# Sparse attention with new orders on four engines, transposes issued one item early, and a bias moved from a one-row product to VectorE

## The chip, the cores and the metric

The kernel runs on one core of a Trainium2 chip. The metric is the device time of one execution in microseconds (us). The core has four engines that compute, each with its own instruction queue, executed in order: TensorE (PE; its weight loads are listed as PEld), VectorE (DVE), ScalarE (ACT) and GpSimd (POOL). SyncE (SP) issues transfers, and so does GpSimd for gathers by index. The engines meet only through semaphores: an instruction waits until a counter has reached a value, and an instruction that is done raises one.

## The reference

4096 tokens of width 128 (16 sequences of 256) pass through four layers, each with a residual sum and a layer norm in front: a linear attention, a mixture of 8 experts (each token goes to one of them), a sparse attention, and the same mixture once more. The sparse attention is the part that changes:

```python
Q, K = (_rope(Q), _rope(K))
iq = (x @ w_iq.T + b_iq).reshape(B, S, IDX_HEADS, IDX_DIM)
ik = x @ w_ik.T + b_ik
iw = x @ w_iw.T + b_iw
head_scores = jax.nn.relu(jnp.einsum('bqhd,bkd->bhqk', iq, ik))
index_scores = jnp.einsum('bhqk,bqh->bqk', head_scores, iw)
_, top_idx = jax.lax.top_k(index_scores, k)      # k = 32 of 256 keys
logits = jnp.einsum('bqd,bkd->bqk', Q, K) * scale + attn_bias   # -inf off the top 32
attn_out = jnp.einsum('bqk,bkd->bqd', softmax(logits), V)
return attn_out @ w_o.T + b_o
```

`iw` has four values per token, one for each index head. Its bias `b_iw` is what the change adds on another engine.

## The kernel before

All data is float32. The program has five stages: the linear attention (to about 85 us), routing and experts (to 204 us), the sparse attention (212 to about 415 us), routing and experts again (to the end). The sparse attention handles one sequence of 256 tokens (two tiles of 128 rows, index `c`) at a time, as a software pipeline written out by hand. In step `b` the engines work on several items at once, and the order in each queue is the order of the source:

- GpSimd (lines 477 to 496) gathers rows of item `b+2` by index (L447, two transfers of 128 rows), multiplies queries and keys of item `b` by cosine and sine (L481, L483), adds them (`qr`, L488), adds the first two weighted heads of each tile (`head_sum`, L466, twice, called heads 0 and heads 1 below), takes the inverse deviation of a later item (`inverse_std`: `vpe` L458 and `rs` L460), and adds an output bias to X (L493).
- VectorE finds the top 32 by four rounds of a maximum of 8 and a replacement (L1329, L1332). Ahead of the rounds it adds the third and fourth head (L1274, L1280) and masks the logits (L1288). Between the rounds stand small pieces of other items (`beside`): after round 0 the normalised rows `xf` of item `b-3` (L1262) and the shift `nb` of item `b+1` (L1237), which both wait for `rs`, after round 2 the attended rows.
- ScalarE copies projections out of PSUM (L888, with `vb` in L891 and `iw` in L915), takes the exponentials (L901), normalises rows of item `b+1` (`xb`, L864, which waits for `nb`), copies scores through a relu (L927, two pairs, called relu 0 and relu 1 below), and scales two heads by `iw` (L934, called part 0 and part 1).
- TensorE transposes `xb` (L691), projects (L660, L663), makes `iw` with a one-row product of ones and the bias row `rowc` (L712) and two products (L714), multiplies probabilities and values (L724), and makes the index scores (L679, two sets of four products). A relu copy waits for its set of scores (`idx`).

So item `b+1` is normalised in step `b`, and before it is projected it must be transposed by TensorE and copied to `xbT` by ScalarE (L872). X and its normalised rows leave through SP (L341, L343).

The expert stages run 39 incidences of a tile with an expert. VectorE and ScalarE fetch tile and expert numbers into registers in groups of eight, where `opens(st, lag)` (line 306) says so. With lag 2, as on VectorE, it holds in steps 2, 8, 16, 24, 32 and 40 of 41; the load at 32 fetches nine numbers, which last to the end.

Of the kernel before, what the change touches and what calls it, by code (L numbers as in the profile page):

```python
# [10 lines left out]
ALU = mybir.AluOpType  # L11
# [3 lines left out]
P = 128  # L15
# [104 lines left out]
def build(nc, x, w_attn, w_idx, w_experts, b1_cols, b2, w_router, cols, b_out, b_o, b_iw, b_r, consts, out):  # L120
    with ExitStack() as ctx:  # L121
# [28 lines left out]
        rowc = sb("rowc", [1, C * IDX_HEADS])  # L150
# [155 lines left out]
        def opens(st, lag):  # L306

            return (st.base - HEAD) % TURN == 0 or st.base == lag or st.base == T
# [5 lines left out]
        def _(sp):  # L314
# [11 lines left out]
            for c in range(C):  # L326
                sp.dma_start(rowc[:, c * IDX_HEADS:(c + 1) * IDX_HEADS], b_iw).then_inc(ld_w, 16)
# [42 lines left out]
        def _(pool):  # L370
# [31 lines left out]
            for st in steps(pool, B, 3, 7, 4, ahead=1):  # L402
                if st.base in GROUP_STEPS and st.on(-1, B):
                    deviations(GROUP_STEPS[st.base])
                if st.on(1, B):
                    b, r = st.item(1), st.slot(1, 2)
                    pool.wait_ge(ld_w, 80)
# [69 lines left out]
            for s in range(B + 2):  # L477
                b, r = s, s % 2
                if b < B:
                    pool.wait_ge(b_["pje"], 8 * b + 7)  # L480
# [4 lines left out]
                    add_heads(b, r, 0)  # L485
                    pool.wait_ge(b_["rp"], 2 * (b + 1))
                    after(pool, b_["S"], C * (b - 1))
                    pool.tensor_tensor(qr[r][:, :, :], qk[r][:, 0:2, :], qk[r][:, 2:4, :], ALU.add).then_inc(b_["qr"], 1)  # L488
                    add_heads(b, r, 1)
                inverse_std(s)  # L490
                if b < B:
                    pool.wait_ge(b_["xb"], b + 1)
                    pool.tensor_tensor(X[:, b * C:(b + 1) * C, :], X[:, b * C:(b + 1) * C, :],  # L493
                                       bo_bc[:, :].unsqueeze(1).to_broadcast([P, C, D]), ALU.add).then_inc(b_["xo"], 1)
                if b + 3 < B:
                    gather_x(b + 3)
# [4 lines left out]
        def _(pe):  # L501
# [26 lines left out]
            for st in steps(pe, B, 6, 7, 4, ahead=1):  # L528
# [18 lines left out]
                if st.base == 6:  # L547
                    pe.wait_ge(ld_w, 80)
# [102 lines left out]
            keep_clock(KEEP_GATHER, bank[4][:, 0:P])  # L651
            for st in (Step(s) for s in range(B + 4)):
# [32 lines left out]
                if st.on(0, B):  # L685
                    b, r = st.item(0), st.slot(0, 2)
                    pe.wait_ge(b_["xb"], b + 1)
                    after(pe, b_["iwe"], b)
                    after(pe, tails[1]["xfT"], b - 3)
                    for c in range(C):  # L690
                        mm = pe.transpose(bank[5][:, c * P:(c + 1) * P], xb[r][:, c, :], ident)  # L691
                    mm.then_inc(b_["T"], 1)
# [34 lines left out]
                if st.on(0, B):  # L727
                    index_scores(0)
# [17 lines left out]
        def _(act):  # L746
# [129 lines left out]
            for st in (Step(s) for s in range(B + 4)):  # L876
# [41 lines left out]
                if st.on(-1, B):  # L918
                    normalise_b(st, -1)
# [469 lines left out]
```

## Time and profile before

| | |
|---|---|
| median of 3 runs | 567.39 us (567.18 to 570.19) |
| the profiled execution | 566.95 us, of it the span of its records 565.1 us |
| busy, share of the span | PE 451.0 us (80%), DVE 380.0 (67%), ACT 337.2 (60%), POOL 288.4 (51%) |
| mean granted clock of TensorE | 0.922 |
| sparse attention | about 212 to 415 us, 16 steps and the run-out |

Most rows of the next section but one are of the timeline: start in us from the start of the span, duration, engine, source line, operation, output and inputs, sizes, number of instructions merged in the row, and in brackets how long the engine was idle before and who ended it. An engine starts an instruction a little before the one ahead is recorded as done, so ends and starts overlap by up to 0.1 us.

### The profile page before, as it was taken

The numbers are of one execution on the slowest core, as the hardware profiler recorded it, in microseconds if no ns is written. First come the engines' busy times: TensorE is split into PE (matmuls) and PEld (weight loads), VectorE is DVE, ScalarE is ACT, GpSimd is POOL, SyncE is SP. The second block draws the span as 40 slices with busy tenths as digits, with TensorE's granted clock in tenths as the row PEclk, the third lists the DMA queues.
The fourth block names the chain that finished last, engine by engine and source line by source line (L and its number), as shares of the span: only waits on it lengthen the run. The fifth ranks groups of instructions, "written<-read, shape, count | busy, mean of one in ns | idle before, by whom it ended". The sixth has DMA issues, their size and how long they took to land. (4 is left out here: it accounts for less than half of the span.)

```text
span 565.1 us, 11633 instructions
## 1 busy us (share of the span) xinstructions
PE 451.0 (80%) x3048; PEld 390.7 (69%) x3048; DVE 380.0 (67%) x1501; ACT 337.2 (60%) x934; POOL 288.4 (51%) x329
## 2 busy tenths in 40 slices
PE   1789985859999986999889998889647668786991
PEld 1578865859999874676666766667437568676981
DVE  5789976425666622999999999999957234434661
ACT  1568852226776616889999899998521245434650
POOL 5753440454430025987778777775410633665442
PEclk9989995979999989999999999999756969888996
DMA  8942232131331110011111111110111321121110
GB/s 224 288 135 77 74 90 25 44 88 53 99 87 35 34 34 15 9 37 32 28 30 30 42 44 28 30 30 21 36 35 5 84 57 48 56 64 56 39 36 17
DMA packets 45070, 32.42 MB, mean 57 GB/s; under 512 B 13524, under 2 KB 39508, under 8 KB 45012
## 3 DMA queue, kind: packets, MB, share of 16 engines
q1 hardware_dynamic: 39892, 19.11, 12.2%
q0 software_dynamic: 5120, 12.62, 8.5%
q8 instruction: 26, 0.43, 0.3%
q14 instruction: 32, 0.26, 0.2%
HBM read 19.10 MB, written 12.62 MB: 56 GB/s over the span
## 5 line engine op out<-in xcount | busy, mean ns | idle before, releaser
L629 PE MATMUL bank<-X,w 128*128 x624 | 91.0, 292 | 18.3 <-ACT X L834 16.3
L639 PE MATMUL bank<-WE,hT 128*128 x624 | 89.2, 289 | 14.3 <-ACT hT L847 6.8
L427 POOL DMA_INDIRECT big<-rows,gidx x64 | 61.5, 961 | 74.7 <-DVE gidx L1147 28.2
L629 PEld LDWEIGHTS bank<-X,w 128*128 128x128 f32 x624 | 82.0, 205 | 22.3 <-issue 21.9
L639 PEld LDWEIGHTS bank<-WE,hT 128*128 128x128 f32 x624 | 81.3, 203 | 17.0 <-issue 16.9
L834 ACT ACTIVATE X<-bank 128x128 f32<-128x128 f32 x64 | 17.9, 280 | 94.6 <-PE bank L620 60.9
L1179 DVE TENSOR_SCALAR hT<-bank,w 128x128 f32<-128x128 f32 x156 | 47.6, 346 | 39.0 <-issue 12.2
L660 PE MATMUL bank<-xbT,WB 128*128 128x256 f32 x224 | 59.2, 394 | 13.2 <-ACT xbT L872 8.5
L839 ACT ACTIVATE w<-WE 128x644 f32 x78 | 57.5, 738 | 3.1 <-DVE big L1191 2.8
L847 ACT ACTIVATE hT<-bank,w 128x128 f32<-128x128 f32 x156 | 48.7, 367 | 13.4 <-PE bank L629 10.1
L447 POOL DMA_INDIRECT X<-x,pidx x32 | 31.7, 989 | 48.7 <-DMA x<-big 41.2
L660 PEld LDWEIGHTS bank<-xbT,WB 128*128 128x128 f32 x224 | 38.7, 189 | 25.2 <-ACT iq L888 11.1
L1332 DVE MATCH_REPLACE8 wk<-m,wk 128x256 f32<-128x256 f32 x128 | 51.8, 416 | 0.0
L433 POOL DMA_INDIRECT out<-big,gidx x32 | 31.4, 980 | 38.1 <-DVE big L1191 32.5
L1329 DVE MAX8 m<-wk 128x8 f32<-128x256 f32 x128 | 47.9, 419 | 0.0
L1185 DVE TENSOR_TENSOR yb<-bank,w 128x128 f32<-128x128 f32 x78 | 22.6, 289 | 36.3 <-PE bank L639 20.4
L1191 DVE SCALAR_TENSOR_TENSOR big<-yb,gm,big 128x128 f32 x78 | 27.5, 353 | 16.4 <-DVE yb L1185 12.1
L679 PE MATMUL bank<-ik,iq 64*128 64x256 f32 x256 | 37.8, 402 | 0.7 <-ACT big L927 0.7
L466 POOL TENSOR_TENSOR head_sum<-big 128x256 f32<-128x256 f32 x32 | 23.6, 736 | 27.9 <-ACT big L934 27.8
L927 ACT ACTIVATE big<-bank 128x512 f32<-128x512 f32 x64 | 34.7, 594 | 1.1 <-PE bank L679 0.9
L888 ACT ACTIVATE big<-bank,COL 128x256 f32<-128x256 f32 x64 | 29.4, 496 | 0.8 <-PE bank L660 0.7
L934 ACT ACTIVATE big<-big,iw 128x256 f32<-128x256 f32 x64 | 29.3, 511 | 0.6
(161 smaller groups left out, 1026.6 us busy)
## 6 DMA issues: line engine op xcount, KB each, us to landing
WE<-w_experts SPq DMA_DIRECT2D x2, 2048.0 KB, 11.5
rows<-xf SPq DMA_DIRECT2D x32, 128.0 KB, 2.2
rows<-X SPq DMA_DIRECT2D x32, 128.0 KB, 2.7
X<-x SPq DMA_DIRECT2D x4, 512.0 KB, 7.6
x<-big SPq DMA_DIRECT2D x32, 64.0 KB, 1.5
big<-rows,gidx POOLq DMA_INDIRECT x64
WB<-w_idx SPq DMA_DIRECT2D x1, 640.0 KB, 5.7
WE<-b SPq DMA_DIRECT2D x1, 512.0 KB, 12.9
```

The source lines that it names most:

```text
L427: pool.indirect_dma_start(xg[:, j, :], None, rows_dram[n], bass.IndirectOffsetOnAxis(ap=gidx[:, j:j + 1], axis=0)).then_inc(f["g"][j % G_R ...
L447: pool.indirect_dma_start(X[:, t, :], None, x2_dram, bass.IndirectOffsetOnAxis(ap=pidx[:, t:t + 1], axis=0)).then_inc(b_["x"][r], 16)
L629: mm = pe.matmul(bank[r + 2 * (k // 2)][:, k % 2 * P:(k % 2 + 1) * P], w1[st.slot(1, 4)][:, k * P:(k + 1) * P], moving, start=True, stop=True)
L639: mm = pe.matmul(bank[4 + r][:, 0:D], hT[r][:, k, :], WE[:, bass.ds(expert[(s - 2) % TURN], 1), W2_AT + k * D:W2_AT + (k + 1) * D].rearran ...
L660: mm = pe.matmul(to, WB[:, i * D:(i + 1) * D], xbT[r][:, :], start=True, stop=True)
L679: mm = pe.matmul(bank[h % 2][:, h // 2 * S:(h // 2 + 1) * S], iq[r][lo:lo + IDX_DIM, h // 2, c * P:(c + 1) * P], ik[r][lo:lo + IDX_DIM, :] ...
L839: act.activation(w1[st.slot(0, 4)][:, :], WE[:, bass.ds(expert[st.base], 1), 0:W1_LEN].rearrange("p a w -> p (a w)"), ACT.Copy).then_inc(f ...
L847: act.activation(hT[r][:, k, :], bank[r][:, k * P:(k + 1) * P], ACT.Relu, bias=w1[st.slot(1, 4)][:, B1_AT + k:B1_AT + k + 1]).then_inc(f[" ...
L927: act.activation(rel[r][:, c, i::2, :], bank[i][:, :].rearrange("p (h k) -> p h k", h=2), ACT.Relu).then_inc(b_["rel"], 1)
L1179: dve.tensor_scalar(hT[r][:, k, :], bank[2 + r][:, k % 2 * P:(k % 2 + 1) * P], w1[st.slot(1, 4)][:, B1_AT + k:B1_AT + k + 1], 0.0, ALU.add ...
L1329: dve.max(m8[:, c, :], wk[r][:, c, :]).then_inc(b_["v"], 1)
L1332: dve.match_replace(wk[r][:, c, :], m8[:, c, :], wk[r][:, c, :], NEG).then_inc(b_["v"], 1)
```

## The change

- GpSimd: in step `s` the gather for item `s+3`, the inverse deviation of step `s-1` and the bias sum of item `s` come first. Then cosine, sine and `qr`, and both head sums last. Before, the head sums stood around `qr`, and inverse deviation, bias sum and gather (of item `s+3`) ended the step.
- TensorE: the transposes of `xb` for item `b+1` go to bank 4 instead of bank 5, and stand in step `b` between the product of probabilities and values and the first set of index scores. Before, they opened step `b+1`, behind the second set.
- ScalarE: in the last pair of projections the `vb` copy comes after the normalisation of item `b+1` and not before it. `xbT` is copied ahead of relu 1 and not behind it. The `iw` copy is gone.
- `iw` is now VectorE's: `index_weights` adds a bias that was broadcast to all partitions, after round 1. The one-row product is gone.
- `opens` holds for steps up to 32 only, so that the load at step 40 of an expert stage falls away on VectorE.

```diff
-            return (st.base - HEAD) % TURN == 0 or st.base == lag or st.base == T
+            return st.base <= T and ((st.base - HEAD) % TURN == 0 or st.base == lag or st.base == T)
...
-            for c in range(C):
-                sp.dma_start(rowc[:, c * IDX_HEADS:(c + 1) * IDX_HEADS], b_iw).then_inc(ld_w, 16)
+            sp.dma_start(biw_bc[:, :], b_iw.rearrange("a e -> (a e)").partition_broadcast(P)).then_inc(ld_w, 16)
...
             for s in range(B + 2):
                 b, r = s, s % 2
+                if b + 3 < B:
+                    gather_x(b + 3)
+                if s > 0:
+                    inverse_std(s - 1)
                 if b < B:
+                    pool.wait_ge(b_["xb"], b + 1)
+                    pool.tensor_tensor(X[:, b * C:(b + 1) * C, :], X[:, b * C:(b + 1) * C, :],
+                                       bo_bc[:, :].unsqueeze(1).to_broadcast([P, C, D]), ALU.add).then_inc(b_["xo"], 1)
                     pool.wait_ge(b_["pje"], 8 * b + 7)
...
-                    add_heads(b, r, 0)
                     pool.wait_ge(b_["rp"], 2 * (b + 1))
                     after(pool, b_["S"], C * (b - 1))
                     pool.tensor_tensor(qr[r][:, :, :], qk[r][:, 0:2, :], qk[r][:, 2:4, :], ALU.add).then_inc(b_["qr"], 1)
+                    add_heads(b, r, 0)
                     add_heads(b, r, 1)
-                inverse_std(s)
-                if b < B:
-                    pool.wait_ge(b_["xb"], b + 1)
-                    pool.tensor_tensor(X[:, b * C:(b + 1) * C, :], X[:, b * C:(b + 1) * C, :],
-                                       bo_bc[:, :].unsqueeze(1).to_broadcast([P, C, D]), ALU.add).then_inc(b_["xo"], 1)
-                if b + 3 < B:
-                    gather_x(b + 3)
+            inverse_std(B + 1)
...
+            def turn_rows(b, r):
+
+                pe.wait_ge(b_["xb"], b + 1)
+                for c in range(C):
+                    mm = pe.transpose(bank[4][:, c * P:(c + 1) * P], xb[r][:, c, :], ident)
+                mm.then_inc(b_["T"], 1)
+
+            turn_rows(0, 0)
...
-                if st.on(0, B):
-                    b, r = st.item(0), st.slot(0, 2)
-                    pe.wait_ge(b_["xb"], b + 1)
-                    after(pe, b_["iwe"], b)
-                    after(pe, tails[1]["xfT"], b - 3)
-                    for c in range(C):
-                        mm = pe.transpose(bank[5][:, c * P:(c + 1) * P], xb[r][:, c, :], ident)
-                    mm.then_inc(b_["T"], 1)
...
-                    pe.matmul(bank[5][:, S:S + C * IDX_HEADS], ones[0:1, :], rowc[:, 0:C * IDX_HEADS], start=True, stop=False)
+                    after(pe, tails[1]["xfT"], b - 3)
...
+                if st.on(-1, B):
+                    turn_rows(st.item(-1), st.slot(-1, 2))
                 if st.on(0, B):
                     index_scores(0)
...
                 if st.on(0, B):
-                    projected(3)
-                    act.wait_ge(b_["pj"], 5 * (b + 1))
-                    after(act, b_["wk"], C * (b - 1))
-                    act.activation(iw[r][:, :, :],
-                                   bank[5][:, S:S + C * IDX_HEADS].rearrange("p (c h) -> p c h", c=C),
-                                   ACT.Copy).then_inc(b_["iwe"], 1)
+                    projected(3, (0,))
                 if st.on(-1, B):
                     normalise_b(st, -1)
+                if st.on(0, B):
+                    projected(3, (1,))
...
-                    if c == C - 1 and st.on(-1, B):
-                        turned(st.item(-1), st.slot(-1, 2))
...
+                    if c == 0 and st.on(-1, B):
+                        turned(st.item(-1), st.slot(-1, 2))
...
+            def index_weights(b, r):
+
+                dve.wait_ge(b_["pj"], 5 * (b + 1))
+                dve.tensor_tensor(iw[r][:, :, :], bank[5][:, S:S + C * IDX_HEADS].rearrange("p (c h) -> p c h", c=C),
+                                  biw_bc[:, :].unsqueeze(1).to_broadcast([P, C, IDX_HEADS]), ALU.add).then_inc(b_["iwe"], 1)
...
+                    if i == 1 and st.on(0, B):
+                        index_weights(st.item(0), st.slot(0, 2))
```

On GpSimd, a middle step of the attention and the opening of the next read so before (`big` is where queries, keys and weighted heads lie, `pidx` the gather's indices):

```order
L466 TENSOR_TENSOR head_sum<-big 128x256 [waits b_s1,b_prt]
L488 TENSOR_TENSOR qr<-big 128x512 [waits b_S,b_rp]
L466 TENSOR_TENSOR head_sum<-big 128x256 [waits b_s1,b_prt]
L458 TENSOR_TENSOR vpe_1<-mv_1,eps 128x4 [waits b_xb,b_mv]
L460 TENSOR_TENSOR rs_1<-vpe_1,mhalf 128x4 [waits b_ve]
L493 TENSOR_TENSOR X<-X,bo_bc 128x256 [waits b_xb]
L447 DMA X<-x,pidx 128x128 [waits b_x0]
L447 DMA X<-x,pidx 128x128
L481 TENSOR_TENSOR big<-big,cst 128x512 [waits b_pje]
L483 TENSOR_TENSOR big<-big,cst 128x512
```

And in the changed kernel, from the same sums on (its line numbers differ):

```order
L493 TENSOR_TENSOR qr<-big 128x512 [waits b_S,b_rp]
L465 TENSOR_TENSOR head_sum<-big 128x256 [waits b_s1,b_prt] x2
L446 DMA X<-x,pidx 128x128 [waits b_x0]
L446 DMA X<-x,pidx 128x128
L457 TENSOR_TENSOR vpe_0<-mv_0,eps 128x4 [waits bt_xf,b_xb,b_mv]
L459 TENSOR_TENSOR rs_0<-vpe_0,mhalf 128x4 [waits b_ve]
L484 TENSOR_TENSOR X<-X,bo_bc 128x256 [waits b_xb]
L487 TENSOR_TENSOR big<-big,cst 128x512 [waits b_pje]
L489 TENSOR_TENSOR big<-big,cst 128x512
```

The two gathers have moved ahead of `vpe` and `rs`, and `qr` ahead of both head sums.

On TensorE, the end of the projections of a middle step before (`prT` are the transposed probabilities, `ik` and `iq` the index keys and queries):

```order
L712 MATMUL bank<-rowc,cst 128x8
L714 MATMUL bank<-WB,xbT 128x4 x2
L724 MATMUL bank<-vb,prT 128x128 [waits bt_lg,bt_x,b_prT]
L724 MATMUL bank<-vb,prT 128x128 x3
L679 MATMUL bank<-ik,iq 128x256 [waits b_rel] x2
L679 MATMUL bank<-ik,iq 128x256 x2
L734 MATMUL bank<-qr 128x256 [waits b_ttr,b_qr]
L734 MATMUL bank<-qr 128x256
```

The same place in the changed kernel:

```order
L714 MATMUL bank<-WB,xbT 128x4 [waits bt_xfT]
L714 MATMUL bank<-WB,xbT 128x4
L724 MATMUL bank<-vb,prT 128x128 [waits bt_lg,bt_x,b_prT]
L724 MATMUL bank<-vb,prT 128x128 x3
L656 MATMUL bank<-cst,xb 128x128 [waits b_xb]
L656 MATMUL bank<-cst,xb 128x128
L687 MATMUL bank<-ik,iq 128x256 [waits b_rel] x2
L687 MATMUL bank<-ik,iq 128x256 x2
L736 MATMUL bank<-qr 128x256 [waits b_ttr,b_qr]
L736 MATMUL bank<-qr 128x256
```

The one-row product is gone, and the transposes of `xb`, which wait for ScalarE's `xb`, stand ahead of the first scores.

On ScalarE, from the seventh projection to part 1 before:

```order
L888 ACTIVATE big<-bank,COL 128x256 [waits b_pj]
L891 ACTIVATE vb<-bank 128x256 [waits b_PV]
L915 ACTIVATE iw<-bank 128x8 [waits b_wk,b_pj]
L864 ACTIVATE xb<-X,nb,rs_1 128x128 [waits b_T,b_nb]
L864 ACTIVATE xb<-X,nb,rs_1 128x128
L927 ACTIVATE big<-bank 128x2x256 [waits b_idx,b_iwe,b_hs]
L927 ACTIVATE big<-bank 128x2x256 [waits b_idx]
L934 ACTIVATE big<-big,iw 128x256 [waits b_rel]
L934 ACTIVATE big<-big,iw 128x256
L751 ACTIVATE xfT<-bank 128x256 [waits bt_T]
L927 ACTIVATE big<-bank 128x2x256 [waits b_idx] x2
L872 ACTIVATE xbT<-bank 128x256 [waits b_idx,b_T]
```

And in the changed kernel:

```order
L890 ACTIVATE big<-bank,COL 128x256 [waits b_pj]
L866 ACTIVATE xb<-X,nb,rs_1 128x128 [waits b_T,b_nb]
L866 ACTIVATE xb<-X,nb,rs_1 128x128
L893 ACTIVATE vb<-bank 128x256 [waits b_PV,b_pj]
L926 ACTIVATE big<-bank 128x2x256 [waits b_idx,b_iwe,b_hs]
L926 ACTIVATE big<-bank 128x2x256 [waits b_idx]
L931 ACTIVATE big<-big,iw 128x256 [waits b_rel]
L931 ACTIVATE big<-big,iw 128x256
L874 ACTIVATE xbT<-bank 128x256 [waits b_idx,b_T]
L753 ACTIVATE xfT<-bank 128x256 [waits bt_T]
L926 ACTIVATE big<-bank 128x2x256 [waits b_idx] x2
```

`xb` now precedes `vb`, the `iw` copy is gone, and `xbT` (L874 there) stands between part 0 and relu 1.

## Rows read from the trace of the kernel before

**Rows 1.** Windows of the attention stage, 240 to 300 us: length, busy time (count).
```profile
240.00:300.00 60.00, 54.03 (x324) 41.15 (x322) 56.75 (x238) 53.10 (x145) 47.36 (x51) 1.00 0.13 31
```

**Rows 2.** Timeline, ScalarE in one step: start us, duration us, line, tiles, idle before.
```profile
302.24 1.09 ACT L927 ACTIVATE big<-bank 128x512 f32<-128x512 f32 x2
...
303.36 0.91 ACT L934 ACTIVATE big<-big,iw 128x256 f32<-128x256 f32 x2
...
304.50 1.09 ACT L927 ACTIVATE big<-bank 128x512 f32<-128x512 f32 x2
...
305.47 0.39 ACT L872 ACTIVATE xbT<-bank 128x256 f32<-128x256 f32 x1
...
305.74 0.92 ACT L934 ACTIVATE big<-big,iw 128x256 f32<-128x256 f32 x2
...
311.58 0.47 ACT L888 ACTIVATE big<-bank,COL 128x256 f32<-128x256 f32 x1
...
312.94 0.39 ACT L891 ACTIVATE vb<-bank 128x256 f32<-128x256 f32 x1 [0.88 <-PE bank L724]
...
313.28 0.88 ACT L864 ACTIVATE xb<-X,nb,rs 128x128 f32<-128x128 f32 x2
...
314.08 1.09 ACT L927 ACTIVATE big<-bank 128x512 f32<-128x512 f32 x2
```

**Rows 3.** Timeline, TensorE before and after that copy (PE, and PEld for weight loads).
```profile
312.83 1.13 PE L679 MATMUL bank<-ik,iq 64*128 64x256 f32 x8
...
316.49 0.20 PEld L691 LDWEIGHTS bank<-cst,xb 128*128 128x128 f32 x2 [0.55 <-issue]
```

**Rows 4.** Timeline of the first steps: TensorE's scores and the ScalarE copies.
```profile
221.06 1.13 PE L679 MATMUL bank<-ik,iq 64*128 64x256 f32 x8
...
222.28 1.09 ACT L927 ACTIVATE big<-bank 128x512 f32<-128x512 f32 x2 [0.17 <-PE bank L679]
...
231.69 1.09 ACT L927 ACTIVATE big<-bank 128x512 f32<-128x512 f32 x2 [0.16 <-issue]
...
243.26 1.09 ACT L927 ACTIVATE big<-bank 128x512 f32<-128x512 f32 x2
```

**Rows 5.** Timeline, GpSimd in the same step.
```profile
305.04 1.27 POOL L488 TENSOR_TENSOR qr<-big 128x512 f32<-128x512 f32 x1
...
306.73 0.73 POOL L466 TENSOR_TENSOR head_sum<-big 128x256 f32<-128x256 f32 x1 [0.43 <-ACT big L934]
...
307.70 1.19 POOL L460 TENSOR_TENSOR rs<-vpe,mhalf 128x4 f32<-128x4 f32 x1
...
308.88 0.82 POOL L493 TENSOR_TENSOR X<-X,bo_bc 128x256 f32<-128x256 f32 x1
...
309.87 1.04 POOL L447 DMA_INDIRECT X<-x,pidx  x1 [0.17 <-issue]
...
312.19 1.28 POOL L481 TENSOR_TENSOR big<-big,cst 128x512 f32<-128x512 f32 x1
```

**Rows 6.** Timeline, VectorE in the same step.
```profile
305.56 1.02 DVE L1274 SCALAR_TENSOR_TENSOR wk<-big,iw,head_sum 128x256 f32<-128x256 f32 x1
...
307.50 0.48 DVE L1274 SCALAR_TENSOR_TENSOR wk<-big,iw,head_sum 128x256 f32<-128x256 f32 x1
...
310.47 0.60 DVE L1262 TENSOR_SCALAR xf<-X,mv,rs 128x128 f32<-128x128 f32 x2
...
310.97 0.17 DVE L1237 SCALAR_TENSOR_TENSOR nb<-mv,rs 128x2 f32<-128x2 f32 x1
```

**Rows 7.** Timeline of the first stage, VectorE beside GpSimd.
```profile
40.66 1.00 DVE L1012 TENSOR_SCALAR xa<-X,mv,r 128x128 f32<-128x128 f32 x2
...
40.84 0.74 POOL L409 TENSOR_TENSOR xres<-xres,bout_bc 128x256 f32<-128x256 f32 x1 [2.36 <-ACT xres L783]
```

**Rows 8.** Timeline, end of the first expert stage.
```profile
199.63 2.24 PE L639 MATMUL bank<-WE,hT 128*128 x16
...
203.40 0.16 DVE L1171 TENSOR_TENSOR gm<-big,mine 128x1 f32<-128x1 f32 x1 [1.82 <-issue]
```

More of the change, by code:

```diff
@@ L149, in build @@
         bv_rep = sb("bv_rep", [P, P])
-        rowc = sb("rowc", [1, C * IDX_HEADS])
+        biw_bc = sb("biw_bc", [P, IDX_HEADS])
         br_bc = sb("br_bc", [P, E])
@@ L406, in _ @@
                     b, r = st.item(1), st.slot(1, 2)
-                    pool.wait_ge(ld_w, 80)
+                    pool.wait_ge(ld_w, 64)
                     pool.wait_ge(a_pt, b + 1)
@@ L547, in _ @@
                 if st.base == 6:
-                    pe.wait_ge(ld_w, 80)
+                    pe.wait_ge(ld_w, 64)
                 if st.on(6, B):
@@ L711, in _ @@
                     b, r = st.item(0), st.slot(0, 2)
-                    pe.matmul(bank[5][:, S:S + C * IDX_HEADS], ones[0:1, :], rowc[:, 0:C * IDX_HEADS], start=True, stop=False)
+                    after(pe, tails[1]["xfT"], b - 3)
                     for c in range(C):
                         mm = pe.matmul(bank[5][:, S + c * IDX_HEADS:S + (c + 1) * IDX_HEADS], xbT[r][:, c * P:(c + 1) * P],
-                                       WB[:, 9 * D:9 * D + IDX_HEADS], start=False, stop=(c == C - 1))
+                                       WB[:, 9 * D:9 * D + IDX_HEADS], start=True, stop=True)
                     mm.then_inc(b_["pj"], 1)
@@ L871, in turned @@
                 after(act, b_["idx"], 2 * C * (b - 1))
-                act.activation(xbT[r][:, :], bank[5][:, 0:S], ACT.Copy).then_inc(b_["xbT"], 1)
+                act.activation(xbT[r][:, :], bank[4][:, 0:S], ACT.Copy).then_inc(b_["xbT"], 1)
             normalise_b(Step(0), 0)
@@ L877, in _, with projected @@
                 b, r = st.item(0), st.slot(0, 2)
-                def projected(pair):
+                def projected(pair, which=(0, 1)):
                     act.wait_ge(b_["pj"], 5 * b + pair + 1)
-                    for i in (2 * pair, 2 * pair + 1):
+                    for i in (2 * pair + w for w in which):
                         src = bank[2 + pair % 2][:, i % 2 * S:(i % 2 + 1) * S]
```

## Prediction

> **What bounds the kernel now.** I read the busy windows first, then the timeline of one step, engine by engine, and followed which event released which. In the attention stage no engine is idle for long: of 60 us DVE is busy 56.8, PE 54.0, ACT 53.1, POOL 47.4, at full clock [rows 1]. So a step is set by a loop of waits. Its length is the distance between two relu 0 copies: 302.24 to 314.08, that is 11.84 us [rows 2]; I read the same distance from step to step in the middle of the stage. All times t below count from relu 0.
>
> In this step ACT waits 0.88 us ahead of `vb` (t = 10.70), runs `xb`, 0.88 long, from 11.04 to 11.92, and goes straight on with the next relu 0 [rows 2]. The reader is to see that TensorE is no slower. Its first scores begin at 312.83, 1.25 us ahead of relu 0 [rows 3], and in the first step, where ACT waited for them, the distance was 1.22 [rows 4]. Both ways to relu 0 end within 0.03 us.
>
> POOL has slack: `rs` is ready at 308.89, but DVE comes to `xf` at 310.47, and `nb` is done at 311.14, 2.1 us ahead of its reader `xb` at 313.28 [rows 2, 5, 6].
>
> **The change part by part.** First the gain that is visible. With `vb` behind `xb`, `xb` could use the wait of 0.88 us, if `nb` is there. It would need `nb` by t = 9.8 (end of the seventh projection: 311.58 + 0.47, t = 9.81 [rows 2]).
>
> Then what stands in its way. The chain is now relu 0, part 1, heads 1, gather, `rs`, `xf` and `nb`, `xb`, transposes, scores, next relu 0. Every link is a wait or an order in the queue rows of the changed kernel, and all of it lies within one step. Its length, link by link:
>
> - Relu 0 to the end of part 1: 306.66 - 302.24 = 4.42 before. Part 0 begins 1.12 after relu 0, but part 1 begins 1.24 after relu 1, with `xbT` in between [rows 2]. Moved ahead, `xbT` costs its 0.27 (305.47 to 305.74) before relu 1, and part 1 then follows at 1.12. That is 0.15 more: 4.57.
> - Heads 1 begins 0.07 later and takes 0.73; two gathers follow, with 0.17 ahead of the first (309.70 to 309.87) and 2.32 from there to the next operation (312.19). `vpe` and `rs` end 1.43 after heads 1 in the old order, so I take 1.47 behind a gather with its start [rows 5]. Sum 4.76: `rs` is ready at t = 9.33. Before it was ready at 6.65.
> - A wait of 0.03, then `xf` and `nb`, 310.47 to 311.14: 0.67 [rows 6]. Then `xb` with 0.04 + 0.88.
> - Transposes: about 0.05 until they start and 0.25 of TensorE's time, by their 0.20 of weight loads [rows 3]. Then 1.22 from scores to relu 0 [rows 4].
>
> Sum: 9.33 + 0.70 + 0.92 + 0.30 + 1.22 = 12.47 us for a step, 0.63 longer than now, with no contention at all.
>
> Next, contention between DVE and POOL. A sum of two SBUF tensors on DVE (L1274) took 1.02 us beside POOL's `qr`, and 0.48 later in the same step, beside `vpe` and the start of `rs`, which have only four elements a row. It ended at 306.58, 0.27 after `qr` [rows 5, 6]. In the first stage a pair of L1012, the same operation as `xf` and of the same size, took 1.00 instead of `xf`'s 0.60 beside a POOL sum [rows 6, 7]. The Trainium skill, "SBUF — State Buffer", section "Who interferes with whom", says that this port pair is an exclusive lock and not a shared bandwidth; by that rule, the trace agrees. Today `xf` meets only a gather, and POOL's bias sum (308.88) is over by then. In the changed order `rs` is followed on POOL by this very sum, at t = 9.31. `xf` arrives at 9.36 and waits until the sum ends, about 10.04 (0.73, as heads 1). The first half of `xf` is done 0.08 later (as 41.66 after 41.58 [rows 7]), the second 0.26 later, `nb` 0.07 after that: 10.45 instead of 10.03. The step is then 12.88 us, 1.04 longer than now. I take this value; without the lock it is 0.63. On the gain side, `qr` no longer holds up L1274, 0.54 us per step on DVE, and hidden, since DVE then has time to spare: it is busy for 56.8 of 60 us [rows 1], so 11.2 of a step, less 0.54, plus some 0.1 for `index_weights`: 10.8 against 12.9.
>
> Without the gather, in steps 13 and 14, the way over TensorE decides: transposes in front of the scores (0.25) and the 0.15 above, on a path that had 0.03 to spare. That is 0.4 per step. The removed one-row product lies in front of the product with the probabilities, which waits for the `prT` copy anyway. I cost it at nothing; without that cover it would give back up to 0.2 a step, since it is about as large as the pair of transposes. The `iw` copy stands in the 0.34 between `vb` and `xb` and is worth 0.1 at most. DVE's replacement comes long before TensorE and ACT ask for it. The weights of `b_iw` need one transfer instead of two, long before use: nothing.
>
> Steps at the start: relu 0 stood 9.41 and 11.57 us apart in steps 1 and 2 (222.28, 231.69, 243.26 [rows 4]), without ACT's `xfT` copy and with shorter `rs`. The new chain is shorter there too, by about 1.0, so about 11.9: 2.5 more in step 1 and 0.4 in step 2 (12.9 at most, the full chain; 11.3 at least, without the lock). Step 0 now has `xb` of item 1 ahead of its first scores: 0.8, an estimate between 0.3 (the transposes alone) and 1.2 (`xb` in full). Step 3 is 1.2 longer, since the distance before was still a little short.
>
> The sum: 0.8 + 2.5 + 0.4 + 1.2 + 9 x 1.04 (steps 4 to 12) + 2 x 0.4 = 15.1 us more.
>
> The load that falls away in `opens`: at the end of an expert stage DVE sat idle for 1.82 us ahead of the last gating product, at 203.40, while TensorE's last products had ended at 199.63 + 2.24 = 201.87. The following sum of the expert bias needs only these, and started 0.08 after 203.40. So it starts 1.6 us earlier [rows 8]. The second expert stage ends with the same pattern: two places, 3.2 us less. It can be 0, if something else ends as late; nothing in the rows says so, since the stores and the last scatter wait for this very result.
>
> Together 15.1 - 3.2 = 11.9 us more. The profiled execution took 566.95 us with a span of 565.1; the median of the runs is 0.44 above it. 567.39 + 11.9 = 579.3, so 579.
>
> **The rivals.** Half a per cent (2.8 us) is about what a measurement can tell from no change.
>
> - No contention: the chain is right but `xf` and `nb` slip in beside the bias sum. 0.8 + 1.9 + 0 + 0.8 + 9 x 0.63 + 0.8 = 10.0, less 3.2: 574. Against it stand rows 5 to 7.
> - The lock is taken again between the halves. POOL's cosine product is ready when the seventh projection is out (t = 9.81 + 0.15, plus 0.07), just when the bias sum ends at 10.04. In the first stage the POOL sum started 0.18 after the pair of DVE, and the pair still ended only with it, so it went between the two halves [rows 7]. If cosine (1.28 [rows 5]) gets in between the halves of `xf`, the step is 14.0, ten steps give about 11 more: 590. If sine then gets in before `nb`, 15.2 and 602. The Trainium skill, "SBUF — State Buffer", section "SBUF: two separate sides", says that the one that starts first holds the pair for its whole instruction; this fits either order and would give 579 to 602.
> - Faster, on the other side: `nb` comes in time, `xb` fills ACT's 0.88 us, and the transposes hide. This decides if `rs` is ready by t = 9.1 less the lock, and if the scores start no later than now. A step of 11.2 over 13 steps gives 8 less, with 3.2 from the load: 556. For it speaks that the idle time is real; against it that the gathers alone add 2.5 us to a path with 2.1 us of slack, and that TensorE had 0.03.
> - The terms cancel, within half a per cent: the transposes cost nothing, the gathers overlap with waits, and only the start loses: about 568.
>
> **How the numbers follow.** One lock per step, 579: 0.38. No contention, 574: 0.14. Cosine in between, 590: 0.18. Sine too, 602: 0.10. Faster, 556: 0.14. Cancelling: 0.06. The range 571 to 603 holds the first four, 0.80. Slower by over half a per cent is their sum too.
>
> **What would show it.** Right: relu 0 every 12.9 us in steps 3 to 12 and every 12.2 in 13 and 14; ACT's `xb` waits for `nb`, and PE's transposes for `xb`; `xf` about 1.0 long right behind `rs`, with two gathers ahead of `vpe`; L1274 back at 0.48; the last gating product of both expert stages right behind TensorE. Wrong: `xb` starting without a wait, or `xf` at 0.6 (574), or 2.3 and more (590 on). If relu 0 comes sooner than 12.4 after the last, one of the links above is not serial.

## Result and the profile after

The changed kernel takes 623.64 us (median of 4 runs, 621.44 to 625.38) against 567.28 us of the kernel before on the same chip (4 runs, 566.59 to 570.19): ratio 1.098, 95% interval 1.093 to 1.103. The direction was forecast, the size was not: 579 with a range to 603. The profiled execution took 623.91 us, span 622.0 us.

The page of the changed kernel: busy time, then two of its costliest groups (busy and mean ns of one, then idle time just before them and what ended it).

```profile
PE 471.9 (76%) x3016; PEld 400.3 (64%) x3016; DVE 397.7 (64%) x1517; ACT 339.0 (54%) x918; POOL 288.1 (46%) x329
...
L465 POOL TENSOR_TENSOR head_sum<-big 128x256 f32<-128x256 f32 x32 | 23.2, 725 | 83.9 <-ACT big L931 83.9
...
L866 ACT ACTIVATE xb<-X,nb,rs 128x128 f32<-128x128 f32 x32 | 14.0, 487 | 39.8 <-DVE nb L1236 39.8
```

POOL's and ACT's busy time stay as they were. PE is busy for 21 us more with 32 instructions fewer, DVE for 18 us more. So the time went into waits, into slower matmuls, and into something that counts as busy on DVE (below it turns out to be waiting inside instructions). The windows of the attention stage (length, busy us and count of PE, PEld, DVE, ACT, POOL, then the granted clock, DMA share, GB/s) show where:

```profile
240.00:300.00 60.00, 43.96 (x232) 32.03 (x232) 49.38 (x180) 41.71 (x108) 37.09 (x40) 0.92 0.09 23
300.00:360.00 60.00, 44.62 (x230) 32.65 (x227) 44.86 (x163) 39.20 (x103) 33.18 (x37) 0.86 0.08 23
360.00:420.00 60.00, 43.65 (x210) 31.04 (x211) 48.01 (x173) 36.08 (x93) 32.17 (x34) 0.80 0.09 25
```

Before, the first of these windows held 324 matmuls at clock 1.00 and no idle engine [rows 1]. Now it holds 232, every engine has slack, and the clock is below 1. The waits of the stage, 212 to 450 us (total us, times, longest):

```profile
POOL head_sum L465 <- ACT big L931: 82.2, 30, 4.6
ACT xb L866 <- DVE nb L1236: 39.8, 12, 11.2
...
ACT big L926 <- PE bank L687: 37.7, 26, 2.6
...
DVE xf L1267 <- POOL rs L459: 10.6, 10, 1.1
```

These waits are links of the forecast loop: part 1, `rs`, `nb`, `xb`, scores, relu. The timeline (start, duration, idle before) shows the end of the first expert stage and then one loop, from relu 0 at 314.64 to relu 0 at 330.81:

```profile
200.48 2.24 PE L639 MATMUL bank<-WE,hT 128*128 x16
...
202.75 0.29 DVE L1184 TENSOR_TENSOR yb<-bank,w 128x128 f32<-128x128 f32 x1 [0.26 <-PE bank L639]
203.25 0.35 DVE L1190 SCALAR_TENSOR_TENSOR big<-yb,gm,big 128x128 f32 x1 [0.20 <-DVE yb L1184]
...
312.45 2.08 PE L687 MATMUL bank<-ik,iq 64*128 64x256 f32 x8
...
314.64 1.08 ACT L926 ACTIVATE big<-bank 128x512 f32<-128x512 f32 x2 [2.59 <-PE bank L687]
...
324.02 1.05 POOL L459 TENSOR_TENSOR rs<-vpe,mhalf 128x4 f32<-128x4 f32 x1
...
325.05 0.71 POOL L484 TENSOR_TENSOR X<-X,bo_bc 128x256 f32<-128x256 f32 x1
...
325.20 1.87 DVE L1267 TENSOR_SCALAR xf<-X,mv,rs 128x128 f32<-128x128 f32 x2 [1.09 <-POOL rs L459]
...
325.74 1.25 POOL L487 TENSOR_TENSOR big<-big,cst 128x512 f32<-128x512 f32 x1
326.95 1.25 POOL L489 TENSOR_TENSOR big<-big,cst 128x512 f32<-128x512 f32 x1
326.99 1.23 DVE L1236 SCALAR_TENSOR_TENSOR nb<-mv,rs 128x2 f32<-128x2 f32 x1
...
328.26 0.88 ACT L866 ACTIVATE xb<-X,nb,rs 128x128 f32<-128x128 f32 x2 [2.67 <-DVE nb L1236]
...
329.19 0.44 PE L656 MATMUL bank<-cst,xb 128*128 128x128 f32 x2 [2.76 <-ACT xb L866]
...
329.56 1.13 PE L687 MATMUL bank<-ik,iq 64*128 64x256 f32 x8
...
330.81 1.09 ACT L926 ACTIVATE big<-bank 128x512 f32<-128x512 f32 x2 [1.40 <-PE bank L687]
```

Read this step against [rows 5, 6]. `xf` took 1.87 us and not 0.60: its second half began when the bias sum ended (L484, 325.76) and ended with cosine (L487). `nb`, two elements a row, took 1.23 us and not 0.17: it ended with sine (L489). Meanwhile TensorE stood idle for 2.76 us. The scores of one step took 2.08 us at the lower of the clock's two levels, 1.2 GHz (312.45), and those of the next 1.13 at the upper, 2.4 GHz (329.56).

The distances between relu 0 copies, in the order of the steps:

| step | 1 | 2 | 3 | 4 to 12 (mean) | 13 | 14 | 15 |
|---|---|---|---|---|---|---|---|
| before | 9.41 | 11.57 | 11.62 | 11.84 | 11.84 | 11.84 | 11.84 |
| forecast | 11.9 | 12.0 | 12.8 | 12.88 | 12.2 | 12.2 | |
| after | 12.11 | 13.35 | 15.85 | 16.92 (16.0 to 17.7) | 13.29 | 12.30 | 11.90 |

The last relu 0 stands 57.8 us later than before (454.73 against 396.95), 1.4 of it already at the first. So the loop takes 56.4 us longer, as much as the times differ by: the loss lies in this loop, and what changed outside of it cancels.

### The profile page after: what moved, and what is told of

Read it like the earlier page. It is cut to its first block and busy times, and to the rows that moved or that the text cites. A ratio compares the mean times of both kernels' runs of the same rounds, so it can differ in the third digit from the quotient of the medians.

```text
span 622.0 us, 11551 instructions
## 1 busy us (share of the span) xinstructions
PE 471.9 (76%) x3016; PEld 400.3 (64%) x3016; DVE 397.7 (64%) x1517; ACT 339.0 (54%) x918; POOL 288.1 (46%) x329
## 5 line engine op out<-in xcount | busy, mean ns | idle before, releaser
L629 PE MATMUL bank<-X,w 128*128 x624 | 89.4, 289 | 11.5 <-ACT X L836 7.6
L629 PEld LDWEIGHTS bank<-X,w 128*128 128x128 f32 x624 | 80.6, 202 | 15.7 <-issue 15.5
L446 POOL DMA_INDIRECT X<-x,pidx x32 | 34.3, 1073 | 47.3 <-DMA x<-big 39.8
L926 ACT ACTIVATE big<-bank 128x512 f32<-128x512 f32 x64 | 34.7, 595 | 38.4 <-PE bank L687 38.4
L687 PE MATMUL bank<-ik,iq 64*128 64x256 f32 x256 | 46.3, 482 | 0.7 <-ACT big L926 0.7
L1190 DVE SCALAR_TENSOR_TENSOR big<-yb,gm,big 128x128 f32 x78 | 27.5, 353 | 16.0 <-DVE yb L1184 12.3
L687 PEld LDWEIGHTS bank<-ik,iq 64*128 64x128 f32 x256 | 28.2, 232 | 12.1 <-issue 7.1
L866 ACT ACTIVATE xb<-X,nb,rs 128x128 f32<-128x128 f32 x32 | 14.0, 487 | 39.8 <-DVE nb L1236 39.8
```

Source lines behind the costliest of these rows:

```text
L446: pool.indirect_dma_start(X[:, t, :], None, x2_dram, bass.IndirectOffsetOnAxis(ap=pidx[:, t:t + 1], axis=0)).then_inc(b_["x"][r], 16)
L629: mm = pe.matmul(bank[r + 2 * (k // 2)][:, k % 2 * P:(k % 2 + 1) * P], w1[st.slot(1, 4)][:, k * P:(k + 1) * P], moving, start=True, stop=True)
L687: mm = pe.matmul(bank[h % 2][:, h // 2 * S:(h // 2 + 1) * S], iq[r][lo:lo + IDX_DIM, h // 2, c * P:(c + 1) * P], ik[r][lo:lo + IDX_DIM, :] ...
L926: act.activation(rel[r][:, c, i::2, :], bank[i][:, :].rearrange("p (h k) -> p h k", h=2), ACT.Relu).then_inc(b_["rel"], 1)
```

## The experiments

All experiments ran on other chips than the run above, where the kernel before takes 529 us. No trace of the kernel before was kept there. The version that differs from it in the bias alone (below) has steps of 11.83 us, as before. Its other stages are shorter: the first relu 0 stands at 210.12 and not 222.28, and 139.9 us follow the last and not 168.2. So the experiments are compared by ratio, and by step.

**The freed register load alone.** The kernel before with one edit:

```diff
-            return (st.base - HEAD) % TURN == 0 or st.base == lag or st.base == T
+            return st.base <= T and ((st.base - HEAD) % TURN == 0 or st.base == lag or st.base == T)
```

> The kernel before with the change of opens alone: VectorE makes no load at step 40 of the two expert stages. By my reading the last gating product of each stage starts 1.6 us earlier: 567.3 - 3.2 = 564 us. If something else ends as late, 567.

Measured: 526.45 us against 529.04, ratio 0.9945 (0.9919 to 0.9972), so 2.6 us less, with 3.2 inside the interval. The step stays at 11.83. The term was right, and it is the only part of the change that was seen to pay.

**The new GpSimd order alone.** The kernel before, with only GpSimd's queue of the changed kernel:

```diff
+                if b + 3 < B:
+                    gather_x(b + 3)
+                if s > 0:
+                    inverse_std(s - 1)
...
-                    add_heads(b, r, 0)
...
+                    add_heads(b, r, 0)
                     add_heads(b, r, 1)
-                inverse_std(s)
```

> The kernel before with the new order on GpSimd alone. Theory of the loop (heads 1, gather, rs, xf and nb taking turns with GpSimd's sums, xb, relu 0): rs is ready at t = 9.2 after relu 0, nb some 3.3 later because bias sum, cosine and sine get in between, xb follows, and relu 0 comes 0.8 after the start of xb without a transpose ahead of it. A step of about 13.5 us, so 567 + 10 x 1.6 + about 3 at the start = 586 us, xf near 1.9 us and nb near 1.2 us long. Rival, that the transposes ahead of the scores and not GpSimd's order carry the loss: 567 to 570 and xb without a wait.

Measured: ratio 1.021 (1.015 to 1.027). Steps 4 to 12 are 12.67 us on average and jump between 12.0 and 13.2 to 13.3. Two steps from its timeline, one of each kind:

```profile
332.49 0.72 POOL L485 TENSOR_TENSOR X<-X,bo_bc 128x256 f32<-128x256 f32 x1
...
332.69 0.86 DVE L1263 TENSOR_SCALAR xf<-X,mv,rs 128x128 f32<-128x128 f32 x2
...
333.34 1.34 POOL L488 TENSOR_TENSOR big<-big,cst 128x512 f32<-128x512 f32 x1
333.48 1.22 DVE L1238 SCALAR_TENSOR_TENSOR nb<-mv,rs 128x2 f32<-128x2 f32 x1
...
344.86 1.88 DVE L1263 TENSOR_SCALAR xf<-X,mv,rs 128x128 f32<-128x128 f32 x2
...
346.65 1.23 DVE L1238 SCALAR_TENSOR_TENSOR nb<-mv,rs 128x2 f32<-128x2 f32 x1
```

The 13.5 us expected were too much. In the first of the two steps, 0.13 us lie between the end of the bias sum (333.21) and cosine, which waits for the seventh projection (its copy ended at 333.27). The second half of `xf` is under way by then and ends at 333.55; here cosine pays, with 1.34 us instead of 1.26. Only `nb` meets a whole sum, and relu 0 comes at 335.52, 12.0 after the last. In the second step the projection is out before the bias sum ends, cosine follows at once (345.39), and `xf` and `nb` pay 1.3 and 1.1 us. What makes the steps alternate was not tried. Here relu 0 follows `xb` directly, 0.78 us after its start (334.74, 335.52), since the transposes still stand in the next step: the two parts of the change cost more together than each alone.

**The new orders with the old GpSimd queue.** The changed kernel, with GpSimd's queue as before:

```diff
-                if b + 3 < B:
-                    gather_x(b + 3)
-                if s > 0:
-                    inverse_std(s - 1)
...
+                inverse_std(s)
...
+                if b + 3 < B:
+                    gather_x(b + 3)
```

> The changed kernel with GpSimd in its old order; all else of the change stays. Theory of the loop: no gather ahead of rs, no sum beside xf, so only the transposes ahead of the scores and the copy of xbT ahead of relu 1 are left, 0.4 us a step: about 12.2 us a step, 567.3 - 3.2 + 6 + 1 = 571 us. Rival, that the early transposes carry the loss: still above 600 us. If the swap of vb and xb gains what ScalarE waited: below 560 us.

Measured: ratio 1.011 (1.006 to 1.016), step 12.29 to 12.30 us, clock 1.00. In its timeline:

```profile
293.51 0.15 DVE L1235 SCALAR_TENSOR_TENSOR nb<-mv,rs 128x2 f32<-128x2 f32 x1
...
295.75 1.13 PE L686 MATMUL bank<-ik,iq 64*128 64x256 f32 x8
...
297.00 1.09 ACT L925 ACTIVATE big<-bank 128x512 f32<-128x512 f32 x2 [1.10 <-PE bank L686]
```

`nb` is early, `xb` doesn't wait, yet relu 0 now waits 1.10 us for TensorE. So the new orders of TensorE and ACT, with the transposes ahead of the scores, cost 0.46 us a step by themselves, near the 0.4 of the prediction. If the early `xb` gives some of it back, it isn't seen.

**No turns between VectorE and GpSimd.** The changed kernel, where GpSimd holds its bias sum until `nb` is done:

```diff
+                if s > 0 and b + 1 < B:
+                    pool.wait_ge(b_["nb"], b + 2)
```

> The changed kernel, but GpSimd waits for nb before its bias sum, so that no sum of it runs beside xf and nb; the gathers stay ahead of rs. Theory that the lock is the larger part: xf back at 0.6 us and nb at 0.17, 2.3 us a step off the loop, TensorE idle for less and so its clock higher, a step of 12.7 to 13.5 us, 580 to 588 us. Rival, that the gathers are the larger part and xf and nb are only shown long: above 605 us.

Measured: ratio 1.025 (1.019 to 1.030), step 12.71 us. The timeline:

```profile
308.26 0.60 DVE L1269 TENSOR_SCALAR xf<-X,mv,rs 128x128 f32<-128x128 f32 x2 [1.08 <-POOL rs L459]
...
308.78 0.15 DVE L1238 SCALAR_TENSOR_TENSOR nb<-mv,rs 128x2 f32<-128x2 f32 x1
...
308.97 0.88 ACT L868 ACTIVATE xb<-X,nb,rs 128x128 f32<-128x128 f32 x2 [0.31 <-DVE nb L1238]
309.01 0.73 POOL L486 TENSOR_TENSOR X<-X,bo_bc 128x256 f32<-128x256 f32 x1 [0.89 <-DVE nb L1238]
```

One added wait on GpSimd takes some 43 us out of the changed kernel (ratio 1.106 in the run below). `xf` and `nb` are as short as before [rows 6], TensorE waits 0.39 us for `xb` and not 2.76, and the granted clock is 1.00 from 250 to 380 us: the wait removes both effects at once. The step is 0.24 above the 12.47 that the prediction added up for a loop without contention.

**The changed kernel again**, unaltered, beside the two that follow:

> The changed kernel as it is, beside the kernel before on one chip, since the earlier experiments ran where the kernel before takes 529 us. With the wait of e4 a step took 12.71 us; without it xf and nb are 1.3 and 1.1 us longer, so the loop is 2.4 us longer by the lock, and what is beyond (16.2 to 17.5 us were seen) is TensorE's lower granted clock. So 541 + 24 + 10 to 20: 575 to 585 us, ratio 1.09 to 1.10. If the first comparison was a matter of its chip, ratio near 1.03.

Measured: 584.59 us against 528.67, ratio 1.106 (1.100 to 1.113), steps of 16.0 to 17.7 us, granted clock 0.84 from 250 to 380 us. The loss is the same 56 us here, so it belongs to the kernel and not to a chip.

**TensorE kept busy.** The changed kernel, with 24 transposes of a constant into a bank that the next transposes overwrite, put where TensorE waits for `xb`:

```diff
+                if st.on(2, B) and st.on(-1, B):
+                    keep_clock(24, bank[4][:, 0:P])
                 if st.on(-1, B):
                     turn_rows(st.item(-1), st.slot(-1, 2))
```

> The changed kernel with 24 transposes of the identity on TensorE, about 2.6 us, in its wait for xb; they end before xb does. Theory that the loop is lengthened once more by the clock: clock at 1.00 in the stage, scores to relu 0 at 1.25 us again, a step of 15.0 to 15.3 us, and 10 to 20 us less than the changed kernel beside it. Rival, that the waits alone give 16 us and more: the same time as the changed kernel.

Measured: 573.2 us, ratio 1.083 (1.076 to 1.090), clock 1.00 from 250 to 380 us. The steps are 15.08 to 15.10 us, all alike. The timeline of one, which began with relu 0 at 302.32:

```profile
310.61 1.04 POOL L459 TENSOR_TENSOR rs<-vpe,mhalf 128x4 f32<-128x4 f32 x1
...
311.64 0.71 POOL L484 TENSOR_TENSOR X<-X,bo_bc 128x256 f32<-128x256 f32 x1
...
311.79 0.65 DVE L1269 TENSOR_SCALAR xf<-X,mv,rs 128x128 f32<-128x128 f32 x1 [1.09 <-POOL rs L459]
...
312.33 1.26 POOL L487 TENSOR_TENSOR big<-big,cst 128x512 f32<-128x512 f32 x1
...
312.87 2.78 PE L514 MATMUL bank<-cst 128*128 128x128 f32 x24
313.56 1.26 POOL L489 TENSOR_TENSOR big<-big,cst 128x512 f32<-128x512 f32 x1
313.60 1.24 DVE L1238 SCALAR_TENSOR_TENSOR nb<-mv,rs 128x2 f32<-128x2 f32 x1
...
314.87 0.88 ACT L868 ACTIVATE xb<-X,nb,rs 128x128 f32<-128x128 f32 x2 [2.69 <-DVE nb L1238]
```

Idle work of 2.78 us a step makes the kernel 11.4 us faster. From step 3 to 12 it gains 17.2 us (150.7 against 167.9), and gives part back elsewhere, as in steps 13 and 14 (14.73 and 14.72 against 13.44 and 12.29). So the rest of the loss beyond 15.1 us a step is the clock.

**`nb` ahead of `xf`.** The changed kernel, with the small instruction first in VectorE's queue:

```diff
-                    if i == 0 and st.on(3, B):
-                        xf_b(st)
                     if i == 0 and st.on(-1, B):
                         shifts(st, -1)
+                    if i == 0 and st.on(3, B):
+                        xf_b(st)
```

> The changed kernel with nb ahead of xf on VectorE. If lock turns go instruction by instruction, nb now waits for the bias sum alone and the halves of xf take the turns after it: nb is out 0.8 us after rs, a step of about 13.0 us, near e4 (ratio 1.03), while xf and not nb is the long one. If xf's own lateness is what costs, the time stays that of the changed kernel.

Measured: ratio 1.044 (1.038 to 1.050), steps of 13.2 and 14.2 us in turn. The timeline:

```profile
300.97 0.69 DVE L1236 SCALAR_TENSOR_TENSOR nb<-mv,rs 128x2 f32<-128x2 f32 x1 [0.99 <-POOL rs L459]
...
301.59 2.59 DVE L1267 TENSOR_SCALAR xf<-X,mv,rs 128x128 f32<-128x128 f32 x2
...
305.54 0.15 DVE L1242 TENSOR_TENSOR iw<-bank,biw_bc 128x8 f32<-128x8 f32 x1
...
305.78 0.60 ACT L926 ACTIVATE big<-bank 128x512 f32<-128x512 f32 x1 [2.93 <-DVE iw L1242]
```

`nb` now pays for one turn only, and ACT's `xb` starts at 301.70. But `xf` pays for two, 2.59 us, and behind it on VectorE stands `iw`, for which relu 0 waits 2.93 us. I had priced that queue at nothing. The granted clock was 0.92 from 250 to 380 us; its share of this step was not parted from that of `iw`. The size was missed (1.03 expected), the turns instruction by instruction were as expected.

**The gathers later.** The changed kernel, with the two gathers between `qr` and the head sums:

```diff
-                if b + 3 < B:
-                    gather_x(b + 3)
...
                     pool.tensor_tensor(qr[r][:, :, :], qk[r][:, 0:2, :], qk[r][:, 2:4, :], ALU.add).then_inc(b_["qr"], 1)
+                    if b + 3 < B:
+                        gather_x(b + 3)
                     add_heads(b, r, 0)
```

> The changed kernel with one thing moved: GpSimd's two gathers stand between qr and the head sums and no longer ahead of vpe and rs. Same output. Theory (the first wait that went wrong is rs coming late, and it comes late through the gathers; the rest is what follows from it): rs ends about 2.1 us sooner, at 7.2 after relu 0 and not at 9.3, the bias sum is over long before cosine may start at about 9.9, so the two halves of xf meet at most the bias sum and are 0.6 to 1.1 us together, nb follows at 0.2, xb starts without a wait for nb, TensorE stays at full clock, and the step is 12.3 us as with the old GpSimd order, about 5 us more in all less the 3 of the loads: ratio 1.00 to 1.02. Rival 1 (the new order of qr and the head sums is what hurts, by turns of VectorE's sums with qr): the step stays above 12.7, ratio above 1.025. Rival 2 (the gathers, now ahead of heads 0, only shift the same delay into the sums of heads, and relu 0 or VectorE's first weighted sum waits for them): step 13 or more with DVE wk waiting for head_sum.

Measured: 540.49 us against 529.11, ratio 1.023 (1.019 to 1.027). The timeline of a step that began with relu 0 at 289.10:

```profile
294.87 1.04 POOL L459 TENSOR_TENSOR rs<-vpe,mhalf 128x4 f32<-128x4 f32 x1
...
298.27 0.59 DVE L1267 TENSOR_SCALAR xf<-X,mv,rs 128x128 f32<-128x128 f32 x2
...
298.78 0.15 DVE L1236 SCALAR_TENSOR_TENSOR nb<-mv,rs 128x2 f32<-128x2 f32 x1
...
298.96 0.88 ACT L866 ACTIVATE xb<-X,nb,rs 128x128 f32<-128x128 f32 x2
299.03 1.27 POOL L485 TENSOR_TENSOR big<-big,cst 128x512 f32<-128x512 f32 x1 [2.41 <-ACT big L890]
```

`rs` is ready at t = 6.81, `xf` takes 0.59, nobody waits for `nb`, and steps 4 to 12 are 12.3 to 12.5 us at full clock. VectorE waits 0.8 to 1.0 us (once 1.75) for the later head sums, and the step is no longer for it than with the old GpSimd queue, within 0.1 on average. The first theory holds for the loop and both rivals fall: the new place of `qr` and of heads 0 isn't what hurts. Its ratio was missed at the upper end (1.00 to 1.02). Most of what is left over the version with the old GpSimd queue (534.50 us) lies at the start: the first four relu 0 copies span 38.4 us here and 34.3 there. In this stretch the second scores of step 1 took 2.08 us (226.57), and `nb` of step 3 met cosine (1.22 us at 248.18).

**The bias alone.** The kernel before, with only the part of the change that concerns `b_iw`:

```diff
-                    pe.matmul(bank[5][:, S:S + C * IDX_HEADS], ones[0:1, :], rowc[:, 0:C * IDX_HEADS], start=True, stop=False)
...
-                    act.activation(iw[r][:, :, :],
-                                   bank[5][:, S:S + C * IDX_HEADS].rearrange("p (c h) -> p c h", c=C),
-                                   ACT.Copy).then_inc(b_["iwe"], 1)
...
+                    if i == 1 and st.on(0, B):
+                        index_weights(st.item(0), st.slot(0, 2))
```

> The kernel before with the one part that gives the change its name alone: the bias of the index weights is added by VectorE after round 1, with no one-row product and no iw copy on ScalarE. Same output, all orders old. Theory of the prediction (worth nothing to 0.1 us a step, since the product stands ahead of a wait for prT, and the copy lies in the 0.34 us between vb and xb): step 11.7 to 11.9 us, ratio 0.997 to 1.002. Rival (VectorE's queue is so full that one more wait in it costs): step 12.0 or more, ratio above 1.004.

Measured: 529.02 us against 529.11, ratio 0.9997 (0.9975 to 1.0018), steps of 11.82 to 11.83 us. Worth nothing, as expected.

**A version from these findings.** The kernel before with the freed load, `qr` ahead of both head sums, and the first scores ahead of the product of probabilities and values, so that ACT could run `xb`, `iw` and relu 0 before `vb`:

```diff
-                    add_heads(b, r, 0)
...
+                    add_heads(b, r, 0)
...
+                if st.on(0, B):
+                    index_scores(0)
                 if st.on(2, B):
...
-                    projected(3)
+                    projected(3, (0,))
+                if st.on(-1, B):
+                    normalise_b(st, -1)
...
+                    if c == 0 and st.on(0, B):
+                        projected(3, (1,))
```

> A version made from the readings: the kernel before with the change of opens, qr ahead of both head sums on GpSimd, the first scores ahead of the product with the probabilities on TensorE, and on ScalarE the order seventh projection, xb, iw, relu 0, vb. Transposes and GpSimd's inverse deviation, bias sum and gather stay where they were. ScalarE's wait of 0.88 us is then filled, TensorE's scores are 1.1 us earlier, VectorE loses no 0.54 us beside qr: a step of 11.0 to 11.3 us instead of 11.84, 7 to 11 us less than e1, ratio 0.975 to 0.985. If another wait takes the place: 0.995 as e1.

Measured: 526.75 us against 528.67, ratio 0.9938 (0.9909 to 0.9968): no better than the freed load alone. The step is 11.72 us and not 11.0 to 11.3. Two rows of its timeline:

```profile
306.26 1.13 PE L679 MATMUL bank<-ik,iq 64*128 64x256 f32 x8
...
307.42 1.08 ACT L928 ACTIVATE big<-bank 128x512 f32<-128x512 f32 x2 [0.63 <-PE bank L679]
```

The second scores now stand behind everything that the first ones passed, and relu 1 waits 0.63 us for them; relu 0 waits another 0.20. Filling a wait of 0.88 us was worth 0.1 a step, since the two waits that TensorE now causes take the rest of it back. No version here clearly beats the kernel before with the freed load (0.9938 and 0.9945, with overlapping intervals).

## Why the prediction was wrong in size

The loop of waits was forecast as it is. Two things that lengthen it were not: VectorE met three GpSimd sums in a row in each step and the sum of the prediction has one, and TensorE's clock fell, which had no term at all. In ten steps (from relu 0 of step 2 to that of step 12, all on one chip, where the kernel before takes 529 us) the parts add up so:

| kernel | ten steps, us | more than the row above |
|---|---|---|
| freed load alone (orders of before) | 118.0 | |
| new orders, old GpSimd queue | 122.6 | 4.6: transposes ahead of the scores |
| new GpSimd queue, held until `nb` | 126.7 | 4.1: `rs` behind the gathers |
| the changed kernel, TensorE kept busy | 150.7 | 24.0: VectorE and GpSimd in turns |
| the changed kernel | 167.9 | 17.2: TensorE's clock |

Step by step of the prediction:

- The loop and its links: right. With TensorE kept busy, part 1 ended at t = 4.48 (forecast 4.57) and `rs` was ready at t = 9.33, the forecast to the hundredth. To the hundredth is luck: part 1 came 0.09 sooner, the first gather took 0.23 longer (1.27), and `rs` took 1.04 and not 1.19. The pieces without contention make 12.71 where 12.47 was added up.
- Where it failed: the step that took **one** lock wait per step, "the second" half of `xf` "0.26 later, `nb` 0.07 after that: 10.45". Measured with TensorE kept busy: first half done at t = 10.12, second at 11.35, `nb` at 12.52. This is the rival that the prediction priced at 15.2 us a step and 602 and gave 0.10; the step was 15.10. As a sign of it the prediction gave an `xf` of 2.3 us and more; it was 1.88. The mechanism was named, its size was set by one row of the first stage [rows 7], where GpSimd had a single sum to do. Here it had three in a row, and each of three VectorE instructions ended 0.02 to 0.09 us after one of them (312.35, 313.59, 314.82 against 312.44, 313.67, 314.84). By the prediction's own times cosine was ready when the bias sum ended. That should have decided for the rival.
- What was missing altogether: TensorE's clock. All durations of PE came from a stage at clock 1.00 [rows 1], while the same forecast made TensorE wait for `xb` in each step. With waits of some 2.76 us in the step the clock fell to 0.92, 0.86 and 0.80 in three successive windows of 60 us, scores took 2.08 us in steps at the lower level, relu 0 and relu 1 came later, and with them the next `rs`. That carried the step from 15.1 to 16 to 17.7 and the total beyond 603. The Trainium skill, "TensorE: Matmul & The Clock Gate", section "HAM oscillation — how this bites in real kernels", tells of a kernel whose TensorE is throttled again in every wait for a DMA between its bursts of matmuls. The trace agrees in part: the waits here are for `xb`, and the clock didn't fall in every one, since the scores of 312.45 (2.08 us) and of 329.56 (1.13 us) both came behind a wait of some 2.75 us. What decides between the two was not found.
- Steps 1, 2 and 3: 2.7, 1.8 and 4.2 us more, forecast 2.5, 0.4 and 1.2. The first was right. In step 2 `nb` met the bias sum alone (0.69 us at 245.88), but relu 1 stands 3.50 us after relu 0 and not 2.06, which is 1.4 of the 1.8; 0.9 of it is a product ahead of its scores (L736), for which TensorE took 2.07 us (235.65) and in the next step 1.13 (248.97). From step 3 on cosine and sine came between as above (`xf` 1.98, `nb` 1.23 us). The first relu 0 was forecast 0.8 later, less 1.6 by the freed load, and was 1.4 later. From the end of the expert stage, where the load is already counted, it stands 20.44 us away (203.25 to 223.69) against 18.31 (203.97 to 222.28): 2.1 where the sum had 0.8. What this is made of wasn't measured.
- Steps 13 and 14: 1.45 and 0.46 more, forecast 0.4 each. Step 14 was right. Step 13 still began at the lower clock: its relu 1 stands 3.44 us after relu 0 (420.68 and 417.24), against 2.46 in the kernel with TensorE kept busy (304.78 and 302.32).
- Transposes ahead of the scores, 0.4: measured 0.46. The one-row product and the `iw` copy, nothing: measured nothing. The load of `opens`, 3.2 less: the last weighted sum now starts 0.53 us after TensorE's end (L1190, 203.25 against 202.72) and not 2.10 (L1191, 203.97 against 201.87), which is 1.6 in the first expert stage as forecast; the times gave 2.6 with 3.2 inside the interval.
- L1274 (L1279 after) is back at 0.48 beside no `qr`, as said. That this is hidden fits the slack of VectorE in the new loop, but no run shows it by itself.

The exclusive lock that the prediction named is seen from VectorE's side. That the pair of ports is held for a whole instruction, the Trainium skill, "SBUF — State Buffer", section "SBUF: two separate sides", states for a VectorE instruction with two SBUF inputs against a GpSimd one that reads SBUF; `nb` has two such inputs, and the trace agrees: 1.23 us for two elements a row, until the end of sine. From GpSimd's side next to nothing is seen of it: with TensorE kept busy, sine starts 1.23 us after cosine though VectorE's second half ran up to then (312.33, 313.56), and 1.23 with no such neighbour in the run with the later gathers (299.03, 300.26). How VectorE gets its turn between two sums at no cost to GpSimd stays open.

One thing stays open: how far the two effects can be parted. The 24.0 us were measured at full clock; at the lower clock the meeting of `xf` and cosine could shift. The rows of the changed kernel show the same 1.87 and 1.23 us, so I take the parts as they stand.

## What to carry to other kernels

When an order is changed, follow the new loop through every queue and ask what stands behind the late result on each engine: here two gathers ahead of a 1 us `rs` turned a slack of 2 us into a wait, and the wait met three GpSimd sums. Where short VectorE instructions stand beside a row of GpSimd sums and one such meeting was seen to make VectorE wait, price one GpSimd sum for each of them; here a wait on GpSimd until the small result was out gave 43 us back. If a forecast lets TensorE wait in each step (2.76 us here, while 0.39 us did no harm), don't take its durations at full clock from before.

## What the runs showed of the hardware

- VectorE and GpSimd took turns instruction by instruction. A pair recorded as one row (`xf`, 0.60 us) took 0.59 to 0.60 alone, 0.86 beside the bias sum, 1.88 beside bias sum and cosine, and 2.59 beside cosine and sine. GpSimd lost next to nothing: its sums took 0.71, 1.25 and 1.25 us beside VectorE (325.05) and 0.73, 1.27 and 1.27 when held until `nb` was done (309.01). Where a half of `xf` had begun before it, with the new GpSimd order alone, cosine took 1.34 (333.34).
- `nb`, with two elements a row, took 0.15 us alone and 1.23 when it ended with sine: the wait is a GpSimd sum long, however small the instruction that waits.
- Filling TensorE's wait with 2.78 us of useless transposes a step raised the granted clock from 0.84 to 1.00 (250 to 380 us) and saved 11.4 us. The scores took 1.13 us at the upper level and 2.08 at the lower.
- The first of two gathers that GpSimd issued took 1.27 us while VectorE made its weighted sums (at 307.77 with TensorE kept busy, at 303.82 in the changed kernel), and 1.04 beside VectorE's maxima and replacements (at 290.71 with the later gathers). I had not counted it; 0.2 us a step.
